# The first 32 expert blocks loaded ahead of the last batch's scatters, under a count taken on the chip

## What is computed

```python
x = x + attention(layernorm(x))            # 16 query heads, 4 key heads, causal
h = layernorm(x)                           # (4096, 256)
topv, topi = top_k(h @ gate_w.T, 8)
W = zeros(4096, 64).at[rows, topi].set(softmax(topv))
gate, up = split(einsum('nh,eih->nei', h, gu_w))
out = einsum('nei,ehi->nh', silu(gate) * up * W[:, :, None], dp_w)
out = out + sigmoid(h @ g1.T) * shared_expert(h)
x = x + out
```

## Time and profile before

| what | value |
|---|---|
| median of three executions | 1210.2 us |
| the profiled execution: span | 1382.2 us |
| PE busy in the span | 1080.5 us, 78% |
| POOL busy | 722.5 us, 52% |
| DVE, ACT busy | 703.8 us, 647.6 us |
| mean granted TensorE clock | 0.909 |

### The profile page before, as it was taken

How to read it: one execution, slowest core, us unless ns; L and a number is a source line. 1 busy time by engine, 2 the same in 40 slices (tenths; PEclk the granted TensorE clock), 3 DMA queues, 4 the chain that set the end, 5 groups by cost and what they waited for, 6 DMA issues and landing times.

```text
span 1382.2 us, 23533 instructions
## 1 busy us (share of the span) xinstructions
PE 1080.5 (78%) x7305; PEld 833.1 (60%) x7305; DVE 703.8 (51%) x2197; ACT 647.6 (47%) x1586; POOL 722.5 (52%) x953
## 2 busy tenths in 40 slices
PE   3799998888888888889765058887888878787875
PEld 1566666565565656566534047777777767676763
DVE  3476766666666666656525411121245544444447
ACT  2465656555555555655331024444445444444441
POOL 3111225657466564564566735655565565655552
PEclk9699999999999989989877569999999999998996
DMA  2586877212122121122228855555767777776536
GB/s 82 174 288 221 275 256 237 101 48 95 51 84 93 53 90 51 59 102 61 84 93 289 269 172 161 172 169 154 238 233 251 268 268 248 259 243 238 170 138 212
DMA packets 142824, 233.18 MB, mean 169 GB/s; under 512 B 17303, under 2 KB 119910, under 8 KB 137840
## 3 DMA queue, kind: packets, MB, share of 16 engines
q1 hardware_dynamic: 67936, 101.06, 22.7%
q0 software_dynamic: 27600, 69.28, 14.1%
q10 hardware_dynamic: 47168, 61.35, 13.5%
HBM read 107.32 MB, written 132.53 MB: 174 GB/s over the span
## 4 chain that ended last, share of the span: by engine, by line
PE 46%; DVE 16%; another core or an unknown queue 14%; issue 13%; ACT 8%; POOL 1%; DMA 1%; ACTq 0%; SPq 0%; DVEq 0%; POOLq 0%
PE psB L1412 6%; DVE nmax L868 6%; PE psD L1429 5%; PE psv L607 4%; PE ps L511 4%; PE psA L1402 4%; PE ps L558 3%; PE ps L518 3%; PE psp L490 3%; PE psp L504 3%; PE psC L1420 3%; ACT xT L1297 2%; ACT y L1313 2%; PE psq L634 2%
## 5 line engine op out<-in xcount | busy, mean ns | idle before, releaser
L1497 POOL DMA_INDIRECT res_d<-y,dst_i x319 | 320.9, 1006 | 231.9 <-ACT y L1313 117.8
L463 POOL DMA_INDIRECT rows_d<-pay,slot_i x256 | 256.5, 1002 | 75.4 <-issue 73.4
L868 DVE TENSOR_REDUCE nmax<-ps 128x1 f32<-128x512 f32 (+3 forms) x448 | 225.8, 531 | 135.8 <-PE ps L518 93.5
L736 ACT ACTIVATE wgu_s<-ps 128x512 f32<-128x512 f32 x320 | 191.9, 600 | 123.4 <-PE ps L518 91.3
L1216 DVE TENSOR_TENSOR inner<-inner,psB 128x128 f32<-128x128 f32 x160 | 45.8, 286 | 316.8 <-ACT inner L1302 250.5
L1429 PE MATMUL psD<-wdp_s,innerT 128*128 x638 | 174.8, 397 | 21.1 <-ACT innerT L1306 17.6
L1412 PE MATMUL psB<-wgu_s,xT 128*128 x1276 | 179.1, 285 | 1.2 <-ACT xT L1297 0.8
L518 PE MATMUL ps<-mask,ident_b 128*128 128x256 bf16 (+1 forms) x640 | 175.4, 274 | 0.4 <-issue 0.4
L511 PE MATMUL ps<-kT,qT 96*128 96x512 f32 (+3 forms) x512 | 168.3, 391 | 8.1 <-DVE nmax L868 4.8
L558 PE MATMUL ps<-qT,kT 128*128 128x512 f32 (+3 forms) x512 | 165.8, 387 | 4.9 <-ACT wgu_s L736 4.2
L1412 PEld LDWEIGHTS psB<-wgu_s,xT 128*128 128x128 f32 x1276 | 163.9, 201 | 1.8 <-issue 1.2
(11 more groups left out here) (256 smaller groups left out, 1620.0 us busy)
## 6 DMA issues: line engine op xcount, KB each, us to landing
rows_d<-blank ACTq DMA_DIRECT2D x8, 5440.0 KB, 19.3
xg<-rows_d SPq DMA_DIRECT2D x160, 272.0 KB
yk<-res_d SPq DMA_DIRECT2D x28, 1024.0 KB
wgu_s<-wgu_in ACTq DMA_DIRECT2D x8, 1024.0 KB
x_d<-x SPq DMA_DIRECT2D x30, 192.5 KB
xs<-x_d SPq DMA_DIRECT2D x30, 192.5 KB, 2.5
res_d<-y,dst_i POOLq DMA_INDIRECT x319
wgu_s<-x_in SPq DMA_DIRECT2D x32, 128.0 KB, 2.2
```

What stands on the lines that cost most here:

```text
L463: pool.indirect_dma_start(rows_d, bass.IndirectOffsetOnAxis(ap=slot_i[par][:, t, k:k + 1], axis=0), pay[par][:, t, :], None).then_inc(s_sc ...
L736: act.activation(pexp[p % 4][:, s, :], ps2[:, (5 * p + s) % 2, :], ACT.Exp, scale=HEAD_D ** -0.5).then_inc(s_exp, 1)
L868: return dve.tensor_reduce(nmax[u][:, tile, heads[0]:heads[-1] + 1], src, AX.X, ALU.max, negate=True)
L1497: pool.indirect_dma_start(res_d, bass.IndirectOffsetOnAxis(ap=dst_i[:, j % (2 * G):j % (2 * G) + 1], axis=0), y[:, j % Y, :], None, bounds ...
```

## The change

Before batch 7 is allotted, DVE works out each expert's next row in its open block (column 15 of `col`; an expert whose blocks are all full gets a number beyond every row) and compares it with rows 2048 and 4096, the ends of the first 16 and the first 32 blocks. PE adds up over the experts, DVE turns the two sums into two integers: 1536 where no open block lies below the bound, 2048 where one does. SP waits for the even batches' scatters alone, reads the first integer into a register, waits for `s_scat[1]` at that value (1536 is batches 1, 3 and 5) and loads the first 16 blocks; it does the same with the second integer before block 16, and waits for all of `s_scat[1]` before block 32. The clearing of `inner` goes from POOL to DVE, and DVE waits for POOL's clearing of `sh` only before it writes there.

```diff
+EARLY_BLOCKS = 16
+        EARLY = 2
+        below = cst[0:EXPERTS, C_MASK1:C_MASK1 + EARLY]
+        needed = cst[0:1, C_MASK2:C_MASK2 + EARLY].bitcast(I32)
...
+                        if ending(h, par, 1):
+                            pe.wait_ge(e_open, 3)
+                            pe.matmul(psq[0:EXPERTS, 2:2 + EARLY], ones_f[0:EXPERTS, 0:EXPERTS], below,
+                                      start=True, stop=True)
...
+                    if k == 0 and ending(h, par, 1):
+                        dve.wait_ge(s_pool, 12 * b)
+                        dve.tensor_scalar(col[:, 15:16], col[:, 0:1], col[:, 1:2], 2.0 ** 20, ALU.is_ge,
+                                          ALU.mult).then_inc(e_open, 1)
+                        dve.wait_ge(e_open, 1)
+                        dve.scalar_tensor_tensor(out=col[:, 15:16], in0=col[:, 0:1], scalar=col[:, 2:3],
+                                                 in1=col[:, 15:16], op0=ALU.add, op1=ALU.add).then_inc(e_open, 1)
+                        dve.wait_ge(e_open, 2)
+                        dve.tensor_scalar(below, cst[0:EXPERTS, C_BLK + EARLY_BLOCKS:C_BLK + EARLY * EARLY_BLOCKS + 1:
+                                                     EARLY_BLOCKS], col[:, 15:16], None, ALU.is_gt).then_inc(e_open, 1)
...
+                        if ending(h, par, 1):
+                            last_batch = 16 * TILES * TOP
+                            dve.tensor_scalar(below[0:1], psq[0:1, 2:2 + EARLY], 0.5, float(last_batch), ALU.is_gt,
+                                              ALU.mult).then_inc(e_open, 1)
+                            dve.wait_ge(e_open, 4)
+                            dve.tensor_scalar(needed, below[0:1], float(last_batch * (BATCH // 2 - 1)), None,
+                                              ALU.add).then_inc(e_needed, 1)
...
-                for par in range(2):
-                    sp.wait_ge(s_scat[par], 16 * TILES * TOP * BATCH // 2)
+                sp.wait_ge(s_scat[0], 16 * TILES * TOP * BATCH // 2)
+                sp.wait_ge(e_needed, 1)
...
+                    if j % EARLY_BLOCKS == 0 and j // EARLY_BLOCKS < EARLY:
+                        n = j // EARLY_BLOCKS
+                        scattered = sp.value_load(needed[0:1, n:n + 1], min_val=16 * TILES * TOP * (BATCH // 2 - 1),
+                                                  max_val=16 * TILES * TOP * BATCH // 2)
+                        sp.wait_ge(s_scat[1], scattered)
+                    if j == EARLY * EARLY_BLOCKS:
+                        sp.wait_ge(s_scat[1], 16 * TILES * TOP * BATCH // 2)
...
                 dve.wait_ge(s_s2, BATCH * SLOTS)
-                dve.memset(wdp_s[INNER:P, :], 0.0).then_inc(e_wdp_zero, 1)
+                dve.memset(wdp_s[INNER:P, :], 0.0).then_inc(e_padded, 1)
+                for t in range(TILES):
+                    dve.wait_ge(s_x2out[t], 16 * (2 * BATCH - 1) if t < 2 else 16)
+                dve.memset(inner[:], 0.0).then_inc(e_padded, 1)
...
+                    if tile == 0:
+                        dve.wait_ge(e_zero, 1)
...
-                act.wait_ge(e_zero, 2)
+                act.wait_ge(e_padded, 2)
...
-                pe.wait_ge(e_wdp_zero, 1)
+                pe.wait_ge(e_padded, 1)
...
                 pool.memset(sh[:], 0.0).then_inc(e_zero, 1)
-                pool.memset(inner[:], 0.0).then_inc(e_zero, 1)
```

More of the change, by code:

```diff
@@ L81, in build @@
         e_wdp = sem("down_weights_in")
-        e_wdp_zero = sem("down_weights_padded")
+        e_padded = sem("down_weights_and_inner_padded")
+        e_open, e_needed = sem("open_blocks"), sem("scatters_needed")
         waits_met = sem("waits_met")
```

## The result

| | before | after |
|---|---|---|
| median | 1209.45 us (1207.71 to 1210.23, 4 runs) | 1194.47 us (1192.33 to 1195.52, 4 runs) |
| ratio, 95% interval | | 0.9869 (0.9852 to 0.9886) |
| span of the profiled execution | 1382.2 us, in a second profile 1216.3 us | 1190.5 us |

The kernel is 15.0 us faster. The forecast was 15.2 us.

The account below looks back on a forecast made before the run. The scatters' pace on POOL was taken to set the expert stage's start. Between POOL's 12.9 us and the chain's 23 us, nearer POOL, it took 15.2 us: 1210.2 - 15.2 = 1195.0 us, range 1185.3 to 1205.2.

Parts of the forecast that it names:

- The lowest open block is 159, nothing needs to wait: Allotment ahead of batch 7: host count gives block 159 against limit 31, both integers 1536, all 32 blocks may load early.
- What ends last without batch 7 is batch 6's landing, twenty us behind its issue: Ahead of the first load: batch 6 down at about 780.7, register read and wait 0.5 us, load issued at 781.3.
- PE's head start: Start of the expert stage: PE starts at 786.0 instead of 808.98, 23.0 us earlier (20.5 to 24.9).
- The added count costs 1.5 us on POOL: Chain to `slot_i`: five DVE operations and a matmul delay POOL's scatters by 1.5 us, moving only POOL's end.
- POOL is late next, the first output 12.9 us earlier: Start of outputs: POOL is in the scatters until 808.1, so outputs start 12.9 us earlier, not 23.
- Over the stage it depends on who is slower: Expert stage: if the PE and ACT chain is slower, 23 us come through; if POOL's 411.5 us bind, 12.9 us.
- The number: Whole kernel: gain between POOL's 12.9 us and the chain's 23 us, nearer to POOL, 15.2 us; chance 0.50.
- Rival A: Expert stage: PE's chain stays the bound all through, gain 23 us, time 1187; chance 0.25.
- Rival C: Early load: integers are 2048 or PE waits for something else, only the count's cost remains, 1211.7 us; chance 0.07.
- B: Batch 7's scatters: early loads share the engines and hold POOL further, gain 5.4 us (3 to 9), 1205; chance 0.13.
- D: Batch 7's scatters: early loads delay their landing to 20 us behind issue, slower than before, 1216 us; chance 0.05.

Follow-up runs that it names:

- the roots are off POOL: After, without POOL's landing wait and `sh` clearing, and with the last batch's four reciprocal roots moved to DVE and ACT: 1186.89 us, ratio to before 0.9812.
- the kernel with full waits: After, with both integers always 2048, so the count is made but the first load waits for all scatters: 1210.48 us, ratio to before 1.0005.
- the run with fewer outputs: After, with the last 31 blocks' indirect output DMAs replaced by small direct ones into a spare tensor: 1188.48 us, ratio to before 0.9827.
- POOL late: Six waited-for memsets on POOL ahead of the first output: added to after 1199.88 us, ratio to before 0.9922; added to before 1210.13 us, 1.0001.
- PE late: After, with extra DVE memsets ahead of the signal PE waits for: two gave 1204.00 us, ratio to before 0.9957; one gave 1197.01 us, 0.9892.
- POOL lighter: After, minus POOL's landing wait and `sh` clearing: 1191.78 us; also minus the last batch's roots: 1186.89; also minus batch 6's column operations: 1180.96, again 1182.94.

## Why the prediction was right, point by point

- **The lowest open block is 159, nothing needs to wait.** Right in what counts: the kernel loads early, at 728.10. The number 159 itself is in no trace.
- **What ends last without batch 7 is batch 6's landing, twenty us behind its issue.** Right in kind: SP's first load comes at 728.10, 18.5 us after batch 6's last issue at 709.58. Its two parts were both off, and the misses nearly cancel. By the count that the prediction used (batch 7's 4.46 MB, taken back from queue 0's last bytes), an estimate, batch 6 was down at about 725.2, 15.6 us behind its issue and not 19.4, and the load came 2.9 us later and not 0.5, beyond the bound of 1.6. The same count gives 2.6 to 3.3 us in six of the experiments with early loads, and some 5 to 8 us where the roots are off POOL. How much of it is the register read, and how much a part of batch 6 that lands behind what the count allows, no run separates. From the load to PE's start it took 733.20 - 728.10 = 5.1 us (4.7 forecast, bounds 2.8 to 7), and PE's head start was 22.2 us (23.0).
- **The added count costs 1.5 us on POOL.** Too dear, by the profile: the slots are ready 5.1 us before POOL can begin with batch 7, since it is still busy with batch 6. The time alone does not settle it (within 0.2% of before, and 1.5 us is 0.12%). The step that failed is small; without it POOL's 12.9 us would have stood at 14.4.
- **POOL is late next, the first output 12.9 us earlier.** Right: 13.1 to 13.5 us. What I had left out are the first pairs' gaps on POOL, 3.2 us in the kernel with full waits, none in after.
- **Over the stage it depends on who is slower.** The first profile said PE's chain, and I gave POOL the better chance only because 172 us were missing from the unprofiled executions. Right, and for the reason given: the second profile of before has neither ACT's waits without a releaser nor POOL's long ones. From the first output to the last, POOL takes 1169.7 - 753.9 = 415.8 us, 1.308 for each of the 318 steps (1.29 forecast). The margin was smaller than the forecast's 2.42 against 2.58 us for a pair: 2.42 is PE's shortest step, and in the run with fewer outputs its mean was 2.58.
- **The number.** 15.2 us stood for "between 12.9 and 23, nearer to POOL". As a mechanism it is POOL's 13.1 us plus 3.2 us of start gaps; the two errors, start gaps unseen and the count overpriced, happen to be made good by the blend. POOL's term alone would have given 12.9 us, 1197.3. It is a right number with a loose derivation, and that it came within 0.2 us is luck.
- **Rival A** (PE's 23 us come through) falls by the runs with POOL late, PE late and POOL lighter. ACT's waits at `y` for the outputs to land, 49.9 us in before, are 75.9 us in after over about the same stage. That fits a head start that runs into a full ring, but it doesn't measure the 9 us that did not come through: the wait grows by 26 us while other waits of ACT shrink (at `y` for PE from 50.2 to 37.9 us). The line of after (770 to 1195 us) that answers to the 49.9:

```profile
ACT y L1351 <- DMA res_d<-y,dst_i: 75.9, 59, 6.2
```

- **Rival C** (it doesn't do what it says) falls by the first load, 22 us ahead of the last scatter.
- **Rivals B and D** (scatters held by the early loads) didn't decide: the last 18 scatters are issued 1.27 us apart beside the loads, and POOL clears `sh` 1.94 us behind the last one's end, before the change 1.58. A little of B is there: in the other profiles with early loads that distance is 1.58 to 3.35 us, so the landing comes 0 to 1.8 us later than in before. In the ten us from 726 to 736 the two queues share the engines:

```profile
q0 software_dynamic: 735, 2.09, 58.8%
q1 hardware_dynamic: 1507, 1.55, 46.0%
```

- **DVE's work beside POOL's scatters** holds nothing up that the trace shows: with 1.28 us of DVE in four (the window of after below) POOL has its four scatters and 3.08 us of work, as in the earlier trace rows, where DVE is idle. The Trainium skill, page SBUF — State Buffer, section Who interferes with whom, says that VectorE in a two-port mode and GpSimd block each other for a whole instruction. The operations in this window are five `tensor_tensor`, a `tensor_reduce` and a `tensor_scalar`; no run shows in which mode they ran, so the trace neither bears that rule out nor speaks against it.

```profile
744.00:748.00 4.00, 4.00 (x35) 3.85 (x34) 1.28 (x7) 2.62 (x8) 3.08 (x4) 1.00 0.91 303
```

## To carry to other kernels

When a stage's start moves, look for the engine that is busy with something else until then and has its own queue of work in the new stage: here PE could start 22 us earlier, POOL 13, and 15 to 16 came out, POOL's 13 and the 3 us of gaps that its first outputs no longer have. A buffer between them turns the faster one's head start into waiting for room. A single profile whose span is far above the other executions must not decide which engine is the bound: subtract the waits that have no releaser, or take it again. And when POOL's queue is the bound, each small operation on it is worth its full length, gap included: 4 roots, a memset and a wait were 7.6 us. Look also at how near the next engine is: in the one stretch where POOL did not hold it, PE's chain took 2.58 us for a pair against POOL's 2.6, so the advice ends soon.

## What the runs showed of the hardware that was not expected

- An indirect DMA of 128 rows costs POOL 0.96 us (into `rows_d`, 1088 bytes a row) or mostly 0.98 to 0.99 us (into `res_d`, 1024 bytes with a bound) and 0.30 us to the next. Four of the first kind fit into 4 us with the DMA engines at 0.37 and at 0.91 (the window above). A direct one costs 0.54 us in all.
- One profiled execution of before was 166 us longer than another. The second has none of the first's waits of ACT without a releaser (100.7 and 39.2 us, 46 times, the longest 6.3). What they were is open.
- A memset of DVE that follows another and waits for it through a semaphore began 0.2 to 3.5 us after it. The large one of `wdp_s` had 3.47 us of idle time ahead of it in every profile but the first of before, which has 3.83. Why is open.
